# Attention of a ViT block on Trainium2: stacking split q and k by SBUF copies and running head pairs on the two row halves of TensorE

## The reference

```python
q = split_heads(holo_linear(x, basis_q, phase_q, amp_q))
k = split_heads(holo_linear(x, basis_k, phase_k, amp_k))
v = split_heads(holo_linear(x, basis_v, phase_v, amp_v))
attn = jnp.einsum('bhqd,bhkd->bhqk', q, k) * scale
attn = jax.nn.softmax(attn, axis=-1)
out = jnp.einsum('bhqk,bhkd->bhqd', attn, v)
```

## Time and profile before

| | us |
|---|---|
| median of 3 runs | 2960.3 |
| range of the 3 runs | 2955.33 to 2965.71 |
| the profiled execution, its own time | 2954.87 |
| its span, first to last instruction | 2953.0 |
| start, until the steps begin | about 57 |
| stage A ends at about | 1600 |
| stage B | the rest |

### The profile page before, as it was taken

The page is one execution under the profiler, slowest core; times in us unless marked ns, Lnnn a source line. Parts: engine busy times, 40 slices in busy tenths (PEclk is TensorE's granted clock), DMA queues, the critical chain, the costliest instruction groups (busy, mean ns, idle before and its releaser), DMA issues. The chain is left out here.

```text
span 2953.0 us, 57443 instructions
## 1 busy us (share of the span) xinstructions
PE 2595.7 (88%) x16871; PEld 2124.6 (72%) x16872; DVE 1788.6 (61%) x4711; ACT 1124.9 (38%) x2993; POOL 626.0 (21%) x581
## 2 busy tenths in 40 slices
PE   2689999999999999999996557499999899999999
PEld 2467777777776776767763446377777699999999
DVE  6466767777667777767761787733333345555555
ACT  0135444445454454444452211044444423333332
POOL 1212212112122121121101675500000022222222
PEclk9589999999999999999996555599999999999999
DMA  2000000000000000000000443222222211122211
GB/s 75 8 8 23 20 16 20 23 16 20 17 23 20 16 20 19 20 20 16 16 9 14 160 131 116 93 82 83 84 85 84 78 54 57 57 64 62 59 57 54
DMA packets 88092, 140.13 MB, mean 47 GB/s; under 512 B 13986, under 2 KB 59860, under 8 KB 87764
## 3 DMA queue, kind: packets, MB, share of 16 engines
q1 hardware_dynamic: 74836, 101.99, 11.5%
q0 software_dynamic: 13056, 35.67, 3.7%
HBM read 83.04 MB, written 54.03 MB: 46 GB/s over the span
## 5 line engine op out<-in xcount | busy, mean ns | idle before, releaser
L735 DVE TENSOR_REDUCE mx<-ps 128x1 f32<-128x257 f32 x1024 | 394.5, 416 | 238.4 <-PE ps L385 214.6
L582 ACT ACTIVATE pT<-ps 128x257 f32<-128x257 f32 x1024 | 343.2, 382 | 285.1 <-PE ps L402 283.8
L385 PE MATMUL ps<-km,q 128*128 128x258 f32 x1024 | 351.3, 360 | 46.8 <-DVE mx L735 23.9
L402 PE MATMUL ps<-q,km 128*128 128x258 f32 x1024 | 283.6, 304 | 2.1 <-ACT pT L582 2.1
L385 PEld LDWEIGHTS ps<-km,q 128*128 128x128 f32 x1024 | 197.4, 193 | 118.5 <-DVE mx L735 57.2
L928 POOL TENSOR_TENSOR rs<-rs,mhalf 128x2 f32<-128x2 f32 x32 | 22.5, 703 | 1004.3 <-DVE rs L687 1004.3
L402 PEld LDWEIGHTS ps<-q,km 128*128 128x128 f32 x1024 | 192.5, 193 | 46.6 <-issue 28.7
L1564 PE MATMUL ps<-zhi,whi 128*128 128x256 f32 x1056 | 214.2, 284 | 1.5 <-DVE zlo L1632 1.5
L1564 PE MATMUL ps<-zhi,wlo 128*128 128x256 f32 x1056 | 211.1, 281 | 0.0
L1564 PE MATMUL ps<-zlo,whi 128*128 128x256 f32 x1056 | 210.6, 281 | 0.0
L1694 POOL TENSOR_TENSOR mark<-rowid 128x1 f32<-128x1 f32 x33 | 6.5, 197 | 860.4 <-DVE idx L1650 860.4
(11 more groups left out here) (321 smaller groups left out, 6278.8 us busy)
## 6 DMA issues: line engine op xcount, KB each, us to landing
z<-zs SPq DMA_DIRECT2D x140, 128.0 KB, 2.0
ys<-z SPq DMA_DIRECT2D x140, 128.0 KB, 1.9
hb<-hscr SPq DMA_DIRECT2D x66, 256.0 KB
xs<-in_x SPq DMA_DIRECT2D x64, 256.0 KB, 3.9
hscr<-h SPq DMA_DIRECT2D x34, 256.0 KB, 2.1
out<-acc SPq DMA_DIRECT2D x32, 256.0 KB
uu<-in_wu SPq DMA_DIRECT2D x6, 768.0 KB, 5.3
raw<-in_wu SPq DMA_DIRECT2D x6, 768.0 KB, 4.9
```

What stands on the lines that cost most here:

```text
L385: pe.matmul(ps[:, n % 2, 0:NP], q2[p % 2][:, h // 2, t * P:(t + 1) * P], km[p % 2][:, h // 2, h % 2, :], start=True, stop=True).then_inc(m ...
L402: pe.matmul(o, km[p % 2][:, h // 2, h % 2, t * P:(t + 1) * P], q2[p % 2][:, h // 2, :], start=True, stop=True).then_inc(s_ps, 1)
L582: act.activation(pT[:, n // LT, n % LT, :], ps[:, 4 + n % 2, 0:N], ACT.Exp, scale=HD ** -0.5).then_inc(s_ok, 1)
L735: dve.tensor_reduce(mx[:, t, h:h + 1], ps[:, n % 2, 0:N], AX_X, ALU.max, negate=True).then_inc(mx_ok, 1)
```

## The change

- `stack`, both `take_stack` and the selector matrices go. The columns of the q and k weights are permuted when they are prepared, so that the heads lie as the copies need them, and SP stacks q and k by DMAs from SBUF to SBUF (`spread`: 6 per image for q and 6 for k, each of 64 rows of 516 elements into 16 partitions). `q2` and the new `k2` have four buffers instead of two; row 48 and row 112 of `k2` are set to one by DMAs at the start.
- No masked keys: each head's product runs over its own 48 rows (49 for the scores), head pairs on rows 0 to 47 and 64 to 111, each into its own bank.
- The maxima of a pair fill banks 0 and 1 together, VectorE reduces both banks in one instruction (16 a step), and the next pair waits for that reduction. The first pair of a step waits for both CLS copies (`mx_ok` + 2), where before it waited for the first.
- The scores of a pair go through banks 4, 5 and 6 in turn.
- The tiles are no longer cleared at the start, x of the first image is loaded ahead of the constants, and a few tiles are merged.

```diff
-        def stack(j, p, r):
...
-            pe.matmul(ps[:, 6, 0:NP], sel[:, 2 * kind, g % 4, :], hi[p % 2][:, f, :], start=True, stop=False)
-            pe.matmul(ps[:, 6, 0:NP], sel[:, 2 * kind + 1, g % 4, :], lo[p % 2][:, f, :], start=False,
-                      stop=True).then_inc(rep_ps, 1)
...
+        def spread(j, p, n):
+
+            sp.wait_ge(lo_ok, 2 * j + n + 1)
+            to, parts = (q2, k2)[n][p % U], ((qhi, qlo), (khi, klo))[n]
+            for part, places in zip(parts, PLACES[n]):
+                for place in places:
+                    for k in range(2):
+                        row = SLOT2 * k + HD * place
+                        sp.dma_start(to[row:row + HD, :, :].rearrange("d (j w) l -> d j (w l)", w=FT).bitcast(F32),
+                                     part[p % 2][SLOT2 * k:SLOT2 * (k + 1), :, :].rearrange("p w l -> p (w l)").bitcast(F32)
+                                     ).then_inc(stack_in[n], 16)
...
+            if has(b + 2):
+                spread(b + 2, p + 2, 0)
+                spread(b + 2, p + 2, 1)
...
-            pe.wait_ge(mx_ok, m * MXN + n + 1)
-            pe.matmul(ps[:, n % 2, 0:NP], q2[p % 2][:, h // 2, t * P:(t + 1) * P], km[p % 2][:, h // 2, h % 2, :],
-                      start=True, stop=True).then_inc(mx_ps, 1)
+        def maxima(m, p, i):
+
+            t, g = i // G2, i % G2
+            if i == 0:
+                for n in range(2):
+                    pe.wait_ge(stack_in[n], 16 * DMAS * (m + 1))
+            pe.wait_ge(mx_ok, m * MXN + i + 2)
+            for k in range(2):
+                rows = slice(SLOT2 * k, SLOT2 * k + STACKED)
+                last = pe.matmul(ps[:, k, 0:NP], q2[p % U][rows, g, t * P:(t + 1) * P], k2[p % U][rows, g, :], start=True,
+                                 stop=True)
+            last.then_inc(mx_ps, 1)
...
-            o = ps[:, 4 + n % 2, 0:NP]
-            pe.matmul(o, km[p % 2][:, h // 2, h % 2, t * P:(t + 1) * P], q2[p % 2][:, h // 2, :], start=True,
-                      stop=True).then_inc(s_ps, 1)
+            if i == 0:
+                if later(b):
+                    pe.wait_ge(s_ok, b * SN)
+            else:
+                pe.wait_ge(s_ok, b * SN + 2 * i - 1)
+            for k in range(2):
+                rows = slice(SLOT2 * k, SLOT2 * k + STACKED + 1)
+                pe.matmul(ps[:, 4 + (2 * i + k) % 3, 0:NP], k2[p % U][rows, g, t * P:(t + 1) * P], q2[p % U][rows, g, :],
+                          start=True, stop=True).then_inc(s_ps, 1)
...
-            dve.tensor_reduce(mx[:, t, h:h + 1], ps[:, n % 2, 0:N], AX_X, ALU.max, negate=True).then_inc(mx_ok, 1)
+            dve.tensor_reduce(mx[:, t, 2 * g:2 * g + 2], ps[:, 0:2, 0:N], AX_X, ALU.max, negate=True).then_inc(mx_ok, 1)
...
-    MX_AT = [3, 3, 3, 2, 3, 3, 3, 2, 2, 2, 2, 2, 2, 0, 0, 0]
+    MX_AT = [2, 1, 2, 1, 1, 1, 2, 1, 1, 1, 1, 1, 1, 0, 0, 0]
...
-        for t in (*qhi, *qlo, *khi, *klo, *q2, *km, *negr):
-            dve.memset(t[:].bitcast(F32), 0.0)
+        for t in negr:
+            dve.memset(t[0:NH, :].bitcast(F32), 0.0)
```

More of the change, by code:

```diff
@@ L150, in stage_a @@
     klo = [sb("klo%d" % p, [P, FT, NP], F32R) for p in range(2)]
-    q2 = [sb("q2_%d" % p, [P, G2, NP], F32R) for p in range(2)]
-    km = [sb("km_%d" % p, [P, G2, 2, NP], F32R) for p in range(2)]
+    q2 = [sb("q2_%d" % p, [P, G2, NP], F32R) for p in range(U)]
+    k2 = [sb("k2_%d" % p, [P, G2, NP], F32R) for p in range(U)]
     bdh = sb("bdh", [P, 2, FT, P], F32R)
@@ L237, in _ @@
     def _(sp):
-        for dst, src in loads:
-            sp.dma_start(dst[:], src).then_inc(c_load, 16)
         for k in range(2):
@@ L242, in _ @@
                          a["x"][0:1].rearrange("n c l h -> (n c) (l h)")).then_inc(x_in, 16)
+        for dst, src in loads:
+            sp.dma_start(dst[:], src).then_inc(c_load, 16)
         sp.wait_ge(half_ok, 1)
+        for t in k2:
+            for k in range(2):
+                row = SLOT2 * k + STACKED
+                sp.dma_start(t[row:row + 1, :, :].bitcast(F32), oner[0:24, 0:G2 * NP // 24].bitcast(F32)).then_inc(ones_in, 16)
         sp.dma_start(hscr[B], h2[:]).then_inc(h2_out, 16)
+        def spread(j, p, n):
[8 more added lines that the diff above has]
+                                     ).then_inc(stack_in[n], 16)
         def step(b, p):
@@ L313, in mixer_out @@
             for f in range(FT):
-                last = pe.matmul(o, yT[:, f, t * P:(t + 1) * P], outw[:, f, :], start=False, stop=(f == FT - 1),
+                last = pe.matmul(o, rden[:, f, t * P:(t + 1) * P], outw[:, f, :], start=False, stop=(f == FT - 1),
                                  skip_group_check=True)
@@ L328, in resonances @@
             for f in range(FT):
-                last = pe.matmul(ps[0:3 * HARM, 3, 0:N], basT[:, f, :], zT[:, f, :], start=(f == 0), stop=(f == FT - 1))
+                last = pe.matmul(ps[0:3 * HARM, 3, 0:L], basT[:, f, :], zT[:, f, 0:L], start=(f == 0), stop=(f == FT - 1))
             last.then_inc(r_ps, 1)
@@ L340, in heads_qk @@
             for f in range(FT):
-                last = pe.matmul(ps[:, 2 + f, 0:N], Wz[:, n, f * P:(f + 1) * P], rT[:], start=True, stop=True)
+                last = pe.matmul(ps[:, 2 + f, 0:NP], Wz[:, n, f * P:(f + 1) * P], rT[:], start=True, stop=True)
             last.then_inc(qk_ps, 1)
@@ L477, in step @@
                 if has(b):
-                    scores(b, p, 2 * n)
-                if len(todo) > 1:
-                    maxima(b + 1, p + 1, todo[1])
-                if has(b):
-                    scores(b, p, 2 * n + 1)
+                    scores(b, p, n)
                 if n == 1 and has(b + 2):
@@ L486, in step @@
                     heads_qk(b + 2, 0)
-                if n < LAG and has(b + 1):
-                    stack(b + 1, p + 1, RN - LAG + n)
-                if n > LAG and has(b + 2):
-                    stack(b + 2, p + 2, n - LAG)
-                if len(todo) > 2:
-                    maxima(b + 1, p + 1, todo[2])
+                if len(todo) > 1:
+                    maxima(b + 1, p + 1, todo[1])
                 if has(b - 1):
@@ L517, in step @@
                         heads_qk(b + 2, 1)
-                    if n == LAG:
-                        stack(b + 2, p + 2, 0)
                     if n == 15:
@@ L598, in step @@
                     high(b + 2, p + 2, 0)
-                if n < LAG and has(b + 1):
-                    take_stack(b + 1, p + 1, RN - LAG + n)
-                if n > LAG and has(b + 2):
-                    take_stack(b + 2, p + 2, n - LAG)
                 if has(b - 1):
@@ L782, in step @@
                     attn_norm(b + 2, p + 2)
-                if n < LAG and n % 2 == 1 and has(b + 1):
-                    take_stack(b + 1, p + 1, RN - LAG + n)
-                if n > LAG and n % 2 == 1 and has(b + 2):
-                    take_stack(b + 2, p + 2, n - LAG)
                 if has(b - 1):
@@ L828, in _ @@
         dve.wait_ge(d_step, 1)
-        for t in km:
-            for k in range(2):
-                dve.memset(t[SLOT2 * k + 32:SLOT2 * (k + 1), :, k, :].bitcast(F32), 1.0)
         dve.memset(va[0][:, :, :, HD:HD + 1], 1.0)
@@ L859, in _ @@
         chain(dve.tensor_tensor(W[:], tr[:], amp[:], ALU.mult))
-        for n in range(3):
-            last = dve.tensor_copy(Wz[n * HARM:(n + 1) * HARM, n, :], W[n * HARM:(n + 1) * HARM, :])
-        last.then_inc(w_ok, 1)
-        dve.tensor_copy(sel[:], selw[:])
+        for n in range(2):
+            rows = slice(n * HARM, (n + 1) * HARM)
+            for f in range(FT):
+                dve.tensor_copy(Wz[rows, n, f * P:(f + 1) * P].rearrange("p (k d j) -> p k d j", k=2, j=4),
+                                W[rows, :].rearrange("p (j w k d) -> p w k d j", j=4, w=FT, k=2)[:, f])
+        dve.tensor_copy(Wz[2 * HARM:3 * HARM, 2, :], W[2 * HARM:3 * HARM, :]).then_inc(w_ok, 1)
         dve.tensor_copy(eyer[:], eye[:])
```

101 lines of the change are left out of this document (34 added, 67 removed).

## The result

The changed kernel takes 3193.2 us (median of 4 runs, 3183.3 to 3207.7) against 2957.8 for the kernel before on the same chip: 1.080 times as long, 95% interval 1.074 to 1.086. The prediction of 2950 us, and its range up to 2996, are wrong by far. Times here are medians over all executions of a kernel, while ratios leave out those more than 1.5% above its fastest (some of e8, e9 and e10, a single one of 5861 us in e17, and a single one of 4191 us of the kernel before; the two large ones stay unexplained).

The account below looks back on a forecast made before the run. A cross-engine chain was taken to bound the step up to `turn`, mostly TensorE after it. Ordinary steps +35, loop-jump steps -16.5, start -17, fill and drain -10 sum to -8.5 us; forecast 2950 us, range 2880 to 2996.

Parts of the forecast that it names:

- Clock: TensorE idling some 3 us before `turn` lowers its granted clock: +0.5 us per ordinary step, bounds 0 and 1.7.
- second stretch: From `turn` to the end of `mixer_out`, some 32 us, mostly TensorE's: -2.0 us a step, bounds -1.0 and -3.0.
- Pairs on row halves: 64 products become 32 fully overlapping pairs at 0.12 instead of 0.24 us each: 3.8 us less a step.
- Form changes: TensorE changes between full and half forms 41 times a step instead of 23, 0.2 us each: 3.6 us given back.
- z held: Before `turn`, GpSimd's copy starts 0.65 us ahead of z and holds it: +3.1 us per ordinary step on the mean.
- One buffer: Maxima pairs share banks 0 and 1, a 1.16 us loop, hidden except at n = 0 and n = 6.
- rival that let the single buffer bind: VectorE's own work delays maxima reductions at one more place per step: +28 us, 2978 us; chance 0.10.
- DMAs at nothing: SP issues 12 more stacking transfers a step, 8 us in a queue otherwise empty, needed a step later: costed at nothing.
- Start: VectorE's clearing of tiles nearly all goes, so setup starts near 15 instead of 32 us: -17 us, at least -14.
- Fill and drain: In the filling steps one stack at a time goes through bank 6; with the last steps -10 us, bounds -3 and -16.
- Loop jump: In the 6 loop-jump steps z is held already and comes out 0.75 us earlier: -2.75 us each, -16.5 us.
- the clock falls in every step and the halves don't overlap: Slower rival: a pair costs 0.24 us and the clock fall 1.7 us a step instead of 0.5: 2999 us; chance 0.13.

Follow-up runs that it names:

- e8: Changed kernel with x split after z is written and the second maxima pair of n = 0, 2 and 6 put behind that place's other work: 2992.1 us, ratio 1.011.
- e9: e8 with 12 full-row filler products a step in the stretches with few full-row products: 3097.5 us.
- e10: e8 with VectorE's class reductions ahead of the second layer norm's statistics: 3001.9 us.
- e17: e16 with x loaded first, tiles written in full no longer cleared, and the masks' zeros set by GpSimd: 2922.9 us, ratio 0.987.
- e4: Kernel before, with only the maxima and scores products cut to row halves (48, 49 rows), selector products and order kept: 3226.1 us, ratio 1.087.
- e3b: Changed kernel with all 128 rows in both products of a pair, so outputs differ: 3079.0 us.
- e12: e8 with maxima and scores products over all 128 rows, so outputs differ: 2912.0 us, ratio 0.984.
- e2: Changed kernel with one more wait on GpSimd, so x is split only after z is written: 3111.8 us.
- e7: Changed kernel without the 12 stacking transfers a step after the first three steps, so outputs differ: 3192.9 us.
- e16: Kernel before with one more wait on GpSimd, so x is split only after z is written: 2939.1 us, ratio 0.993.
- e18: e17 with the loop over the batch written out in full: 2883.8 us, ratio 0.974.
- e5: e2 with 18 unread filler products a step of 512 columns over all 128 rows, ahead of full-row work: 3136.8 us.
- e6: e5 with each filler taking 48 rows instead of 128, same count, columns and places: 3196.7 us.
- e14: Changed kernel with 64 rows instead of 48 or 49 in each half's product, added rows zero: 3153.1 us.
- e13: e8 with 64 rows instead of 48 or 49 in each half's product, added rows zero: 3033.4 us.

## Why the prediction was wrong

*Clock* is the step that failed. I charged 0.5 us per ordinary step, with 0 and 1.7 as bounds, from one fall of 6.8 us behind one idle stretch. Measured are three falls in the step shown, 30.7 us at the half clock, so some 15 us. The -2 us of the second stretch stood on durations at full clock. Step times clock gives 53.1 us x 0.72 = 38 us at full clock, and 44.5 x 0.98 = 44 for the kernel before. That estimate is a lower bound for the changed kernel, since waits and other engines don't run faster with TensorE's clock; it doesn't show how much shorter the step would be at full clock. What the change took was the selector products, all of 128 rows, and what it put in place of 64 full-row products was 32 pairs of few rows with waits between; the clock then fell in three places of the step shown, none of them brought on by the wait ahead of `turn`. I had looked for the clock only where I knew of an idle wait. My upper bound should have been the whole step at half clock.

*Pairs on row halves*: the overlap was right, the price of a pair wrong even at full clock: 0.23 us to the next start, where I took 0.12, since the next weights are loaded only 0.11 us behind the pair's start. So the 3.8 us a step are not there at all. With the clock the halves are a loss: e4 +261 us, e3b -114 and e12 -80 for going back. *Form changes*: 41 a step as counted (the kernel before has 25, I had 23). At full clock it takes 0.21 to 0.31 us from a full-form product to a pair, where full form to full form takes 0.12, and 0.21 to 0.31 from a pair to another form, where pair to pair takes 0.23 (medians of most pairs of lines that follow each other). So a change adds up to 0.19 going in and up to 0.09 coming out, less than the 0.2 that I took for each. I did not measure their sum apart from the clock.

*z held*: right in mechanism and about right in size, mean 1663 ns from 226 to 1700 us where I said near 2 us; e2 prices it at 81 us. But GpSimd's copy led z by 2.37 us in the step shown, not by 0.65, and had ended, so the subtraction alone held z. *One buffer*: right places (n = 0 with 0.59 us, n = 6 with 1.10), but not n = 2, and I left it to the second stretch's bounds, 1 us either way; e8 got 120 us by hiding these three waits. The rival that let the single buffer bind had the mechanism at 28 us, a quarter of that, since it left the clock out.

*DMAs at nothing*: right (e7). *Start* -17: right; the first mixer product comes at 37.27 (said: 39), and e17 against e16 gives -16.2 for the like. *Fill and drain* -10: the first L726 comes 15 us earlier, where the start alone gives 18, and behind the last one the two kernels take the same time (1396.6 us, 1395.0 before), so filling and draining gained nothing.

*Loop jump* -0.75: wrong in mechanism. I put the low clock of the earlier trace rows to z held there; e16 frees z and the fall stays, e18 removes the jump and the fall goes. The Trainium skill (TensorEngine Tiling (Array Packing), Key Properties) warned of the drains at form changes and pointed the right way. The trace agrees: from the full form to a pair it takes 0.21 to 0.31 us, within the full form 0.12. That the halves themselves cost clock, no row of the kernel before showed: its products of few rows stand in small groups between full-row ones.

The rival "the clock falls in every step and the halves don't overlap" came nearest. It had the falling clock and a pair's price of 0.24 right, and the overlap wrong, and it priced the fall at 1.7 us a step instead of some 15.

## What to carry to other kernels

When a change takes products away from a kernel that is bound by TensorE at full clock, cost the step a second time at the half clock, and ask for every stretch what full-row work is left in it: here 1024 products fewer made the kernel 8% slower. Test pairs on row halves alone first, one slice per product: here a pair took as long as two full-row products even at full clock, and the clock did not hold. Put independent work between two products that share a bank pair, and look at the loop jump: writing the loop out was worth 39 us, more than any edit of the products.

## What the runs showed of the hardware

- Products on row halves hold the clock less well: the same fillers gave a granted clock of 0.88 with 128 rows and 0.82 with 48, in spite of fewer form changes (e5, e6), and the kernel before fell from 0.98 to 0.84 by slicing 128 rows to 48 and 49 (e4). Rows alone, in the same form, gave 0.76 for 0.72 in one pair of kernels (e14) and nothing in another (e13).
- Two halves overlap, but the weights of the next pair are loaded 0.11 us behind the pair's start, where in full form they are loaded with it: 0.23 us from pair to pair, 0.12 from one full-row product to the next.
- In the step shown, stretches at 0.50 of 6.7, 6.7 and 17.0 us follow the thin stretches at once, though TensorE is busy for 6.03, 6.70 and 17.00 us in them.
- Steps lock: most of the changed kernel's steps take 54.2 to 55.2 us one after another, most of e8's 44.4. And the four executions of e8 differ by 2.7% (2959 to 3038 us), where the kernel before, its one outlier aside, stays within 0.6% on one chip.
- A loop jump idles TensorE 2.15 us by "issue" (e16), and written out in full, 36 steps in the program instead of 12, the same work costs nothing that can be measured (e18).
- 12 stacking transfers a step, 0.29 of the DMA engines' time instead of 0.07, cost nothing that can be measured (3193.2 and 3192.9 us, e7).
